# Moving six groups' second-layernorm statistics from VectorE to ScalarE, with x added by an identity product on TensorE

## The reference, cut to what matters

```
x = _layernorm(x + _L0_attn_ref(...))          # x1 below
x = _layernorm(x + _L0_ffn_ref(x, ...))        # the norm that is moved
# _layernorm: (x - mean) / sqrt(var + 1e-5) over the 128 features
```

## Time and profile before

| | |
|---|---|
| median of 3 runs | 527.58 us (526.69 to 528.39) |
| profiled execution, its own time | 531.46 us |
| span of its trace | 529.7 us |
| busy in the span | PE 369.5, PEld 270.4, DVE 444.1, ACT 236.2, POOL 220.0 us |
| mean granted TensorE clock | 0.768 of full speed |

### The profile page before, as it was taken

The page is one execution under the profiler, slowest core; times in us unless marked ns, Lnnn a source line. Parts: engine busy times, 40 slices in busy tenths (PEclk is TensorE's granted clock), DMA queues, the critical chain, the costliest instruction groups (busy, mean ns, idle before and its releaser), DMA issues.

```text
span 529.7 us, 24223 instructions
## 1 busy us (share of the span) xinstructions
PE 369.5 (70%) x10097; PEld 270.4 (51%) x10097; DVE 444.1 (84%) x2770; ACT 236.2 (45%) x371; POOL 220.0 (42%) x311
## 2 busy tenths in 40 slices
PE   5686786418537775786777787847976876778856
PEld 2233474114434555464736484726464656556855
DVE  1537899699999969898999699989998997998643
ACT  3967804426514532463346235632644372345212
POOL 1042420144348751616283428435252747082630
PEclk9989965759655876898778668876886796588878
DMA  8700000000000000000000000000000000000001
GB/s 236 165 0 2 1 1 0 1 1 2 4 2 5 3 2 4 3 4 4 24 2 4 4 24 3 4 22 5 2 5 24 5 3 4 22 4 2 24 6 41
DMA packets 7661, 8.95 MB, mean 17 GB/s; under 512 B 896, under 2 KB 6912, under 8 KB 7424
## 3 DMA queue, kind: packets, MB, share of 16 engines
q1 hardware_dynamic: 6976, 7.34, 5.1%
q10 hardware_dynamic: 576, 0.07, 0.1%
HBM read 5.31 MB, written 2.10 MB: 14 GB/s over the span
## 4 chain that ended last, share of the span: by engine, by line
PE 52%; DVE 20%; issue 17%; ACT 8%; DMA 1%; SPq 0%; ACTq 0%; DVEq 0%
PE psum L880 17%; PE psum L857 16%; PE psum L867 9%; PE psum L837 5%; PE psum L776 4%; DVE arena L669 3%; DVE idx L614 3%; DVE arena L525 2%; DVE x L575 2%; ACT L423 1%; DVE vals L606 1%; DVE arena L673 1%; DVE arena L666 1%; DVE arena L672 1%; DVE picked L638 1%
## 5 line engine op out<-in xcount | busy, mean ns | idle before, releaser
L857 PE MATMUL psum<-arena 64*64 64x16 f16 x8192 | 93.8, 182 | 91.5 <-issue 70.0
L857 PEld LDWEIGHTS psum<-arena 64*64 64x64 f16 x8192 | 87.7, 120 | 110.0 <-issue 104.8
L880 PE MATMUL psum<-ko,arena 64*128 64x128 f32 x1024 | 91.2, 355 | 3.6 <-issue 3.6
L417 ACT ACTIVATE arena<-psum 128x1024 f32<-128x1024 f32 x32 | 32.8, 1024 | 134.0 <-PE psum L857 134.0
L880 PEld LDWEIGHTS psum<-ko,arena 64*128 64x128 f32 x1024 | 88.0, 267 | 4.2 <-issue 3.9
L239 POOL TENSOR_TENSOR cand<-vals 128x128 f32<-128x128 f32 x16 | 13.2, 824 | 169.1 <-DVE vals L606 169.1
L614 DVE FIND_INDEX8 idx<-vals,sims 128x8 uint32<-128x32 f32 x512 | 82.7, 185 | 0.0
L286 POOL TENSOR_TENSOR arena<-arena 128x512 f32<-128x512 f32 x60 | 77.8, 1331 | 4.2 <-ACT arena L417 4.2
L669 DVE TENSOR_TENSOR arena<-iota,listsT 128x4096 f16<-128x4096 f16 x32 | 74.9, 2341 | 0.0
L867 PE MATMUL psum<-x1T,trn 128*64 128x256 f32 x512 | 62.8, 400 | 8.7 <-ACT arena L423 8.7
L837 PE MATMUL psum<-msim,xn 128*128 128x512 f32 x64 | 54.9, 1008 | 4.9 <-ACT xn L375 4.9
(11 more groups left out here) (113 smaller groups left out, 529.5 us busy)
## 6 DMA issues: line engine op xcount, KB each, us to landing
x<-in_L_attn_x_dram SPq DMA_DIRECT2D x8, 256.0 KB, 4.7
out_dram<-nat SPq DMA_DIRECT2D x7, 256.0 KB, 2.3
ko<-in_L_ffn_key_out_dram SPq DMA_DIRECT2D x2, 512.0 KB, 9.5
nat<-in_L_ffn_key_in_dram SPq DMA_DIRECT2D x2, 256.0 KB, 8.0
nat<-in_L_ffn_keys_dram SPq DMA_DIRECT2D x2, 128.0 KB, 5.4
out_dram<-nat SPq DMA_DIRECT2D x2, 128.0 KB, 1.7
nat<-in_L_attn_W_delta_dram SPq DMA_DIRECT2D x1, 64.0 KB, 2.8
nat<-in_L_attn_W_in_dram SPq DMA_DIRECT2D x1, 64.0 KB, 2.7
```

The lines of the kernel that those rows point to most:

```text
L417: act.activation(dst, src, ACT.Copy, scale=1.0 / W_SCALE).then_inc(s["p_evac"], 1)
L857: end = pe.matmul(psum[64 * e:64 * e + 64, at:at + NJ], hotx[rows, g, :, e], hotw[rows, part, g, :, e], start=(part == 0), stop=(part == 1))
L880: end = pe.matmul(y2[:, e, m % 2] if m < NS - 1 else y_last[:, e], gl[rows, m % 4, j, :], ko[rows, j, :], start=(j == 0), stop=(j == NJ - 1))
```

## The change

For groups 0 to 5 `residual(q)` is gone from VectorE. TensorE starts each y2 sum of steps m = 0 to 11 with two products of x1T (x1 transposed, already in SBUF) with the identity, so that y2 holds x1 plus the layer's output. ScalarE gets `z_out(q)` between `lists_out` and `sims_out` of odd steps: four ACTIVATEs that copy y2 to `zf` and add up each token's sum. `spread2(q)`, now behind `signs`, takes minus the mean, four squares of the deviations with their sums, and then the square root. `scales` uses the new minus mean. Groups 6 and 7 keep VectorE's statistics. Other semaphores (`zt_done` for the tail) follow from that. The core of the diff:

```
+            def z_out(q):
+                wait(act, "y2_mm", q * 2 + 2)
+                wait(act, "out_done", q)
+                for t in range(CH):
+                    end = act.activation(zf[:, t, :], y2[:, t % 2, t // 2], ACT.Identity, accum_out=sum2[:, t:t + 1])
+                end.then_inc(s["zf_done"], 1)
+
             def spread2(q):
-                wait(act, "mv2_done", q + 1)
+                wait(act, "zf_done", q + 1)
                 wait(act, "nmr2_done", q)
+                act.mul(nm2[:, :], sum2[:, :], -1.0 / D).then_inc(s["nm2_done"], 1)
+                wait(act, "nm2_done", q + 1)
+                for t in range(CH):
+                    end = act.activation(dev2[:, t, :], zf[:, t, :], ACT.Square, bias=nm2[:, t:t + 1],
+                                         accum_out=ssq2[:, t:t + 1])
+                end.then_inc(s["ssq2_done"], 1)
+                wait(act, "ssq2_done", q + 1)
                 wait(act, "out_done", q)
+                act.activation(rstd2[:, :], ssq2[:, :], ACT.Sqrt, bias=eps[:, 0:1], scale=1.0 / D).then_inc(s["sd2"], 1)
...
+                if m >= 5 and m % 2:
+                    z_out(m // 2 - 2)
                 if m + 1 < NS:
                     sims_out(m + 1)
                 if m + 2 < NS:
                     normed(m + 2)
                 if m % 2 and m < NS:
                     gelus(m // 2)
+                if m < NS:
+                    signs(m)
                 if m >= 5 and m % 2:
                     spread2(m // 2 - 2)
-                if m < NS:
-                    signs(m)
...
                     hots_of(m - 1, 0)
-                    if m >= 5 and m % 2:
-                        residual(m // 2 - 2)
                     if m >= 6 and m % 2 == 0:
                         scales(m // 2 - 3)
                     hots_of(m - 1, 1)
...
             def experts_out(m):
-                wait(pe, "zf_done", m // 2)
+                wait(pe, "zf_done", min(m // 2, NCH - 2))
+                if m // 2 == NCH - 1:
+                    pe.wait_ge(s["zt_done"], 1)
+                to = y2[:, :, m % 2] if m < NS - 1 else y_last
+                with_x = m // 2 < NCH - 2
+                for e in range(2 if with_x else 0):
+                    pe.matmul(to[:, e], x1T[:, m * SW + e * P:m * SW + (e + 1) * P], ident[:, :], start=True, stop=False)
```

More of the change, by code:

```diff
@@ L126, in seqffn_kernel @@
         mv2 = sb("mv2", [P, CH, 2])
+        sum2 = sb("sum2", [P, CH])
+        nm2 = sb("nm2", [P, CH])
+        ssq2 = sb("ssq2", [P, CH])
+        dev2 = sb("dev2", [P, CH, P])
         rstd2 = sb("rstd2", [P, CH])
@@ L156, in seqffn_kernel @@
             wk_done whi_done wlo_done conv_done lists_mm lists_evac hoty_done hot_done
-            p_mm p_evac g_mm gelu_done a_done a_tail y2_mm zf_done st2_done mv2_done sd2 rstd2_done nmr2_done
+            p_mm p_evac g_mm gelu_done a_done a_tail y2_mm zf_done zt_done nm2_done ssq2_done st2_done mv2_done sd2 rstd2_done nmr2_done
             out_done stored""".split()
@@ L425, in gelus, with spread2_tail @@
                                        s["gelu_done"], 1)
+            def z_out(q):
[4 more added lines that the diff above has]
+                end.then_inc(s["zf_done"], 1)
             def spread2(q):
-                wait(act, "mv2_done", q + 1)
+                wait(act, "zf_done", q + 1)
                 wait(act, "nmr2_done", q)
-                wait(act, "out_done", q)
+                act.mul(nm2[:, :], sum2[:, :], -1.0 / D).then_inc(s["nm2_done"], 1)
[5 more added lines that the diff above has]
+                wait(act, "ssq2_done", q + 1)
+                wait(act, "out_done", q)
+                act.activation(rstd2[:, :], ssq2[:, :], ACT.Sqrt, bias=eps[:, 0:1], scale=1.0 / D).then_inc(s["sd2"], 1)
+            def spread2_tail():
+                act.wait_ge(s["mv2_done"], 1)
+                act.wait_ge(s["nmr2_done"], NCH - 2)
+                act.wait_ge(s["out_done"], NCH - 2)
                 act.activation(rstd2[:, :], mv2[:, :, 1], ACT.Sqrt, bias=eps[:, 0:1]).then_inc(s["sd2"], 1)
@@ L442, in spread2_half @@
                 n = slice(2 * u, 2 * u + 2)
-                act.wait_ge(s["mv2_done"], NCH + u)
+                act.wait_ge(s["mv2_done"], 2 + u)
                 act.wait_ge(s["out_done"], NCH - 1)
@@ L484, in _ @@
                     p_out(m - 1, 0)
-            spread2(NCH - 2)
+            spread2_tail()
             p_out(NS - 1, 1)
@@ L673, in hots_of, with residual_tail @@
                 dve.tensor_tensor(hotw[:, 1, at], hoty[:, at], spread(3, NJ), ALU.mult).then_inc(s["hot_done"], 1)
-            def residual(q):
+            def residual_tail():
+                q = NCH - 2
                 wait(dve, "out_done", q)
@@ L679, in residual @@
                                   x1[:, q * CH:(q + 1) * CH, :].rearrange("p (m e) d -> p m e d", e=2),
-                                  ALU.add).then_inc(s["zf_done"], 1)
-                wait(dve, "zf_done", q + 1)
+                                  ALU.add).then_inc(s["zt_done"], 1)
+                wait(dve, "zt_done", 1)
                 for t in range(CH):
@@ L684, in residual @@
                 end.then_inc(s["st2_done"], 1)
-                wait(dve, "st2_done", q + 1)
+                wait(dve, "st2_done", 1)
                 for t in range(CH):
@@ L693, in scales @@
                 wait(dve, "rstd2_done", q + 1)
-                dve.scalar_tensor_tensor(out=nmr2[:, :], in0=mv2[:, :, 0], scalar=-1.0, in1=rstd2[:, :],
-                                         op0=ALU.mult, op1=ALU.mult).then_inc(s["nmr2_done"], 1)
+                if q < NCH - 2:
+                    dve.tensor_tensor(nmr2[:, :], nm2[:, :], rstd2[:, :], ALU.mult).then_inc(s["nmr2_done"], 1)
+                else:
+                    dve.scalar_tensor_tensor(out=nmr2[:, :], in0=mv2[:, :, 0], scalar=-1.0, in1=rstd2[:, :],
+                                             op0=ALU.mult, op1=ALU.mult).then_inc(s["nmr2_done"], 1)
             for m in range(NS + 1):
@@ L719, in last_residual @@
                 dve.tensor_tensor(zf[:, n, :], y2[:, :, 0] if u == 0 else y_last, x1[:, T - 4 + 2 * u:T - 2 + 2 * u, :],
-                                  ALU.add).then_inc(s["zf_done"], 1)
-                dve.wait_ge(s["zf_done"], NCH + u)
+                                  ALU.add).then_inc(s["zt_done"], 1)
+                dve.wait_ge(s["zt_done"], 2 + u)
                 for t in range(2 * u, 2 * u + 2):
@@ L724, in last_residual @@
                 end.then_inc(s["st2_done"], 1)
-                dve.wait_ge(s["st2_done"], NCH + u)
+                dve.wait_ge(s["st2_done"], 2 + u)
                 for t in range(2 * u, 2 * u + 2):
@@ L736, in last_scales @@
                                          op0=ALU.mult, op1=ALU.mult).then_inc(s["nmr2_done"], 1)
-            residual(NCH - 2)
+            residual_tail()
             dve.wait_ge(s["gelu_done"], NCH * JR)
@@ L879, in experts_out @@
                         rows = slice(64 * e, 64 * e + 64)
-                        end = pe.matmul(y2[:, e, m % 2] if m < NS - 1 else y_last[:, e], gl[rows, m % 4, j, :], ko[rows, j, :], start=(j == 0),
+                        end = pe.matmul(to[:, e], gl[rows, m % 4, j, :], ko[rows, j, :], start=(j == 0 and not with_x),
                                         stop=(j == NJ - 1))
```

## The result

The changed kernel took 536.89 us, median of four runs (533.73 to 537.37; a fifth that is listed with them took 539.02), against 527.99 us for the kernel before in the same comparison. The ratio is 1.0164, 95% interval 1.0113 to 1.0215: 8.9 us slower, where 8.1 were forecast. Its profiled execution took 533.73 us, less than the other runs, so the traces show less of the loss (spans 531.9 and 529.7 us) than the medians do; the medians carry the size, the traces the place. Ratios leave out single runs that lie over 1.5% above the fastest of their kernel: four of six in e7_both_moves, four of twelve in e10_no_stats, and one each in e9, e12 and the kernel before of e9 to e11.

What follows compares the result with a forecast made beforehand. The prediction took TensorE to set the pace in odd steps, with VectorE's residual inside its lead. Products 7.5 us plus ScalarE's lateness 0.6 made 8.1 us, so 527.6 became 535.7 us, range 527.5 to 542.5.

Steps and rivals of the forecast that it cites:

- TensorE sets the pace in odd steps, and the residual lies in VectorE's lead: Odd steps: TensorE never waits for VectorE there, so time saved on VectorE becomes waiting for the turned lists.
- The value 0 for the removal: Residual of six groups off VectorE: 0 us taken as gain, -11.5 us if every microsecond counted.
- The identity products, 7.5 us: Two products ahead of twelve experts_out on TensorE: 8.4 us, partly returned by the clock; 7.5 taken, bounds 5.4 to 8.4.
- the bound of 3.0 that I set: experts_out behind the products: shifting it into higher-clock time gives back at most 3.0 us.
- `z_out`, 1.65 us with 0.1 us uncovered: ScalarE ahead of the gelus, odd steps: 1.65 us against 1.57 us of waits, 0.6 us late in all.
- The work behind the gelus, 0: ScalarE's multiply, squares and square root behind the gelus: about 0.3 + 1.65 us, fits the 1.99 us wait, value 0.
- Instruction fetches, 0 with 3 us either way: TensorE's fetch gaps every 256 instructions move to other offsets in the scatter: value 0, 3 us allowed either way.
- the 3 us that the prediction named as a sign of being wrong: Gaps marked "issue" changing by over 3 us in total would show the forecast wrong.
- VectorE as the bound: Rival: VectorE sets the pace, each group gives 1.92 us and products fall into TensorE's waits; 516 us, chance 0.06.
- no change: Rival: products raise the clock sooner, fetch gaps fall better, ScalarE isn't late; 525 to 530.5 us, chance 0.18.
- ScalarE late: Rival: running sums double z_out to 3.3 us, gelus start 1.7 us late in six odd steps; 546 us, chance 0.14.
- 8.1 - 3 - 3 - 3: Milder form of the VectorE rival: products bring the clock up and fetch gaps fall well, leaving about 528.

Runs made afterwards that it cites:

- e7_both_moves: Kernel before with experts_out ahead of the scatter half in even steps and the turned lists' eviction first on ScalarE: 519.08 us, ratio 0.9661.
- e10_no_stats: Kernel before without bn_stats and bn_aggr of six groups on VectorE, the add of x1 kept: 529.81 us, ratio 0.9929.
- e9: Changed kernel with four identity products instead of two in front of experts_out of steps 0 to 11: 544.54 us, ratio 1.0194.
- e12: Kernel before with the whole residual of six groups left out on VectorE, ScalarE and TensorE unchanged: 528.91 us, ratio 0.9977.
- e11: Kernel before with bn_stats of six groups done twice on VectorE, nothing left out: 531.64 us, ratio 0.9991.
- e2: Changed kernel without the identity products, x1 left out of six groups' last norm: 525.57 us, ratio 0.9967.
- e1: Kernel before plus only the identity products in steps 0 to 11, VectorE still adding x1: 534.7 us, ratio 1.0134.
- e5: Changed kernel with experts_out moved ahead of the scatter half in even steps: 521.2 us, ratio 0.9830.
- e4: Kernel before with experts_out moved ahead of the scatter half that waits for one-hots, in even steps from 4: 515.92 us, ratio 0.9766.
- e8: e2 with eight more of z_out's ACTIVATEs with sums, into a spare tile, making z_out three times as long: 540.07 us, ratio 1.0167.

## Why the prediction was right, point by point

**TensorE sets the pace in odd steps, and the residual lies in VectorE's lead.** Right. e12 and e2 give 0.9977 and 0.9967 where VectorE's 11 us would have given 0.979, e11 gives 0.9991, and TensorE's wait for the one-hots stays at 12.6 and 11.3 us where it was 12.0. That VectorE waits longer for the lists is a weaker sign: of the 9.7 us more, e1 has 5.0 without any relief, and e12 has none. The value 0 for the removal may be a few tenths of a per cent short of the truth.

**The identity products, 7.5 us.** Right in sum: e1 gives 7.1 us (5.0 to 9.1). Both of its pieces were mis-sized, and that they cancel is luck. A group of four records takes 1.15 us at half clock, not 0.87, and 0.65 at full clock, not 0.47 (0.54 in e5, behind the scores), and eleven of twelve started at or near half clock, where seven were counted: 13.1 to 13.9 us, not 8.4. The price came from the spacing of a long row of products; why a short group is dearer than that isn't shown. What comes back in the sums behind is 7.3 us in the changed kernel's trace and 4.6 in e1's, not the 0.9 taken, and above the bound of 3.0 that I set. That bound rested on a misreading: the 5.47 us from 235.50 were taken as near full clock, while the granted clock was 0.64 in the first microsecond and 0.68 over the sum. At 1.00 the same 64 records take 3.84 us (e4), so even this sum had 1.6 us to give back. A part of the 7.3 is also the two gaps that left the sums. What stays net is 6.6 us in one trace and 9.4 in the other, and TensorE's whole busy time grew by 5.5 and 6.5.

**`z_out`, 1.65 us with 0.1 us uncovered.** The size was off: 1.0 us, and fully covered. The cover held for one `z_out` (e2) and not for three (e8); its exact size isn't shown.

**The work behind the gelus, 0.** Right: the eviction behind it starts without a wait and not late.

**Instruction fetches, 0 with 3 us either way.** Not settled. TensorE's gaps without a releaser in the ten steps are 45.9 us before and 47.4 after in the two traces, 1.5 us more; over the whole traces they are 79.0 and 75.4, 3.6 us less, which is over the 3 us that the prediction named as a sign of being wrong. The sign was set too narrow: e11 and e12, where TensorE's list is that of the kernel before, have 79.5 and 73.0 us. Offsets did move: the gaps in `experts_out(4)` and `experts_out(10)` are gone, and one of three in the transposes. The fetches were not tested by themselves.

**What should have shown.** VectorE's busy time fell by 9.0 us, a little under the 10 to 12 forecast; TensorE's rose by 5.5, a little under 6 to 9. The four added records took neither 0.47 nor 0.87 us. The distance from lists to lists grew by 1.0 us in the odd pair shown, but by 0.43 a step over ten steps, where 0.8 was forecast; the traces show less of the loss than the medians. The 8.9 us of the medians are 1.8 more than e1's 7.1, within the intervals, so nothing else is needed for the loss.

**The rivals.** VectorE as the bound, and no change, are excluded by the ratio's interval and by e2 and e12. ScalarE late is excluded by e2 and bounded by e8. One reading against the first rival was too strong: VectorE's seven waits for the lists were said to be 2.15 us or longer, and four of them are 1.0 to 2.0 us. And 8.1 - 3 - 3 - 3 leaves 526.7 us, not about 528, which changes no chance.

## What to carry to other kernels

The busiest engine need not be the one to relieve; ask whose wait ends at whom, and whether the work that you move lies inside a lead that shows as a wait a step later. Here 84% busy VectorE waited for lists that TensorE had to turn, and an add moved onto TensorE's list had no wait to hide in: two small matrix products, 1.15 us each time at half clock, cost some 7 us in all. The same reading pointed at TensorE's own wait in even steps, and putting work that was ready in front of it took 2.3% off, more than the change had to offer, much of it because that work then ran at the higher clock. A forecast that takes times from rows has to take the granted clock of the same rows with them.

## What the runs showed of the hardware that was not expected

A running sum on ScalarE is a second instruction, ACTIVATION_READ_ACCUMULATOR: its row is 0.22 to 0.24 us long here, but the next ACTIVATE starts 0.25 us after the one before (PSUM to SBUF, 128 columns), so four tiles with sums take 1.0 us, less than four plain ones with two pointer operands (1.65 us).

Four float32 records with 128 rows in front of a sum take 1.15 us at a granted clock of 0.50 and 0.54 to 0.65 at 1.00, where the same shape in a long row takes 0.22 and 0.117 us a record, 0.87 and 0.47 us for four.

The sum of 64 float32 records takes 3.84 us at a granted clock of 1.00 (e4), 4.98 at 0.75 and 5.47 at 0.68 (the kernel before). Time multiplied by clock gives an estimate of 3.7 to 3.8 us at full clock each time. Where a sum stands in the list was worth over 1 us here through the clock alone.

TensorE's gaps without a releaser add up to 73.0 us in one trace (e12) and 79.5 in another (e11) of the same list of TensorE instructions, 6.5 us or 1.2% of the span, and e10 and e12, which remove nested parts of the same work, came out 0.2% apart in the wrong order by medians and 0.5% by ratios. A difference of that size between two kernels here says little.
